# Causal mask and row minima of one attention head: two instructions over 512 columns in place of four with accumulators

## The reference, cut to what matters

```python
scores = jnp.einsum('bqnd,bknd->bnqk', q, k) * scale
causal = jnp.tril(jnp.ones((s, s), bool))
scores = jnp.where(causal, scores, -1000000000.0)
p = jax.nn.softmax(scores, axis=-1)
attn = jnp.einsum('bnqk,bknd->bqnd', p, v).reshape(b, s, NH * VD)
```

## Time and profile before

| | |
|---|---|
| timed runs, median (all three) | 987.31 us (984.85, 987.31, 988.54) |
| profiled execution, first to last instruction | 989.1 us; what lies around it isn't shown |
| PE busy | 861.2 us, 87% of the span |
| PEld busy | 611.6 us, 62% |
| DVE busy | 794.5 us, 80%, 2309 instructions |
| ACT busy | 664.4 us, 67% |
| POOL busy | 516.8 us, 52% |

### The profile page before, as it was taken

How to read it: one execution, slowest core, us unless ns; L and a number is a source line. 1 busy time by engine, 2 the same in 40 slices (tenths; PEclk the granted TensorE clock), 3 DMA queues, 4 the chain that set the end, 5 groups by cost and what they waited for, 6 DMA issues and landing times. The chain is left out here.

```text
span 989.1 us, 24025 instructions
## 1 busy us (share of the span) xinstructions
PE 861.2 (87%) x8118; PEld 611.6 (62%) x8118; DVE 794.5 (80%) x2309; ACT 664.4 (67%) x1611; POOL 516.8 (52%) x607
## 2 busy tenths in 40 slices
PE   3476689999999898999999899998998579999971
PEld 1243346777767676676767677676765357787740
DVE  4688878888888988989998877778867767777738
ACT  3677878888888877788788676666753136666640
POOL 5778883466466463777745264211453715554540
PEclk8555559999999999999999999999999779999986
DMA  5222320101001010122000223114231534444448
GB/s 183 93 77 75 102 104 23 31 19 43 15 25 30 23 52 1 59 87 71 26 15 9 65 91 119 39 34 134 80 103 46 189 108 150 153 155 148 137 161 316
DMA packets 47493, 83.81 MB, mean 85 GB/s; under 512 B 6144, under 2 KB 36224, under 8 KB 47328
## 3 DMA queue, kind: packets, MB, share of 16 engines
q1 hardware_dynamic: 39504, 61.45, 19.7%
q0 software_dynamic: 6864, 19.80, 5.7%
q10 hardware_dynamic: 1008, 1.03, 0.3%
HBM read 52.77 MB, written 31.85 MB: 86 GB/s over the span
## 5 line engine op out<-in xcount | busy, mean ns | idle before, releaser
L668 PE MATMUL ps<-whi,ar 128*128 128x256 f16 (+1 forms) x797 | 225.9, 283 | 19.0 <-DVE ar L1764 9.4
L670 PE MATMUL ps<-whi,ar 128*128 128x256 f16 (+1 forms) x797 | 225.6, 283 | 0.0
L669 PE MATMUL ps<-wlo,ar 128*128 128x256 f16 (+1 forms) x797 | 225.6, 283 | 0.0
L1543 POOL TENSOR_TENSOR ar<-ar,sm 128x512 f32<-128x512 f32 x64 | 69.8, 1090 | 149.2 <-DVE sm L1833 149.1
L668 PE MATMUL ps<-ar 128*128 128x128 f16 (+1 forms) x768 | 117.4, 207 | 13.0 <-issue 5.3
L1458 POOL TENSOR_TENSOR sm<-sm,mhalf 128x1 f32<-128x1 f32 (+2 forms) x72 | 125.4, 1741 | 6.0
L1594 POOL DMA_INDIRECT y<-ar,idx x79 | 76.0, 962 | 88.3 <-ACT ar L1428 74.4
L669 PE MATMUL ps<-ar 128*128 128x128 f16 (+1 forms) x768 | 117.0, 206 | 0.0
L670 PE MATMUL ps<-ar 128*128 128x128 f16 (+1 forms) x768 | 117.0, 206 | 0.0
L668 PE MATMUL ps<-ar,whi 128*128 128x512 f16 x292 | 114.3, 392 | 0.2
L669 PE MATMUL ps<-ar,whi 128*128 128x512 f16 x292 | 114.2, 391 | 0.0
(11 more groups left out here) (234 smaller groups left out, 2308.0 us busy)
## 6 DMA issues: line engine op xcount, KB each, us to landing
ar<-xg SPq DMA_DIRECT2D x79, 144.0 KB
ar<-in_wall SPq DMA_DIRECT2D x16, 512.0 KB, 3.6
stg<-in_wall SPq DMA_DIRECT2D x32, 188.0 KB, 2.5
ar<-in_wall SPq DMA_DIRECT2D x8, 608.0 KB, 4.3
whi<-y SPq DMA_DIRECT2D x4, 1024.0 KB, 8.1
wlo<-y SPq DMA_DIRECT2D x4, 1024.0 KB, 16.0
xg<-in_pad SPq DMA_DIRECT2D x1, 2304.0 KB
xg<-x1d SPq DMA_DIRECT2D x4, 512.0 KB, 4.7
```

The costliest lines, as they stand in the source:

```text
L668: mm(o, l_hi, r_hi, start=start, stop=False, skip_group_check=True)
L669: mm(o, l_hi, r_lo, start=False, stop=False, skip_group_check=True)
L670: return mm(o, l_lo, r_hi, start=False, stop=stop, skip_group_check=True)
L1543: TT(pr, pr, er4.unsqueeze(2).broadcast_to([P, GB, S]), ALU.mult).then_inc(sem("p_n"), 1)
```

## The change

The four instructions with accumulators become two over all 512 columns: an addition of the mask, repeated over the four batches, and a reduction by minimum over each batch's 128 columns that writes the four columns of `nm4` at once. Between them VectorE waits for the addition by a new semaphore, `m_add`. The semaphore `mask_in` is dropped: the mask's load counts on `idn_in`, behind a wait for the two loads that count there already.

```diff
                     if p == FIRST - 1:
-                        sp.dma_start(msk[:, :], maskb).then_inc(sem("mask_in"), 16)
+                        sp.wait_ge(sem("idn_in"), 32)
+                        sp.dma_start(msk[:, :], maskb).then_inc(sem("idn_in"), 16)
...
             def a_max(g, h):
                 dve.wait_ge(sem("s_ps"), g * NH + h + 1)
                 if g == 0 and h == 0:
-                    dve.wait_ge(sem("mask_in"), 16)
-                for j in range(GB):
-                    c = slice(j * S, (j + 1) * S)
-                    last = V.tensor_tensor_reduce(bank(SB_)[:, c], bank(SB_)[:, c], msk[:, :], 1.0, -MASKED, ALU.add, ALU.min,
-                                                  nm4[:, j:j + 1])
-                last.then_inc(sem("m_neg"), 1)
+                    dve.wait_ge(sem("idn_in"), 48)
+                sc = bank(SB_).rearrange("p (j k) -> p j k", j=GB)
+                TT(sc, sc, msk[:, :].unsqueeze(1).broadcast_to([P, GB, S]), ALU.add).then_inc(sem("m_add"), 1)
+                dve.wait_ge(sem("m_add"), g * NH + h + 1)
+                V.tensor_reduce(nm4, sc, AX.X, ALU.min).then_inc(sem("m_neg"), 1)
```

## The result

The changed kernel took 995.69 us (median of six, 992.82 to 1003.18) against 987.33 us, a ratio of 1.0093 with the interval 1.0062 to 1.0123. Timed a second time, beside the last experiments, it took 999.62 us, ratio 1.0134 (1.0101 to 1.0167). It is slower by about 1%. The profiled execution spans 996.1 us, and 1.9 us lie around it (997.98 us in all).

What follows compares the result with a forecast made beforehand. TensorE was taken to bound the attention stage, paying only where it waits for VectorE work behind the step: 3.8 + 1.4 + 1.1 + 1.6 + 0.6 = 8.5 us, added to the 987.31 median, gives 995.8 us; range 986.5 to 1004.

Steps and rivals of the forecast that it cites:

- The step's price: Each head's mask-and-minimum step: VectorE held 1.34 us instead of 0.96 (0.38 more), minima ready 0.32 us later.
- VectorE not the bound: Attention stage: TensorE sets the pace; 24.3 us more VectorE work over 64 heads, against 86 us of VectorE idle time.
- Late k waits: Last 20 heads: ten k projections waiting for the value split behind the step each grow by 0.38 us, 3.8 us.
- early third heads: Eleven third heads among the first 44: k projection has 0.25 us of cover, 0.13 comes through each, 1.4 us.
- late fourth heads: Fourth heads of the last five periods: value projection behind the q split starts 0.33 us later each, 1.6 us.
- Starts of periods behind the router: Heads 24, 40, 56: scores wait for the k split behind the router's softmax; all 0.38 us comes through, 1.1 us.
- Smaller places: A k/v row ahead of the query projection and a few value projections: 0 to 2 us together, taken as 0.6.
- The rival in which VectorE binds: First 440 us: delays add up, plus collisions; two thirds to all of 24.3 us paid, 1003 to 1012 us; chance 0.12.
- Hidden: Rival: pauses are given back at TensorE's later waits, so no change, 987.3 us give or take 1.5; chance 0.17.
- Faster: Rival: the two passes take 0.35 us each, the step saves 0.30 us, total 984 us; chance 0.09.
- The mask's load at nothing: Mask load on another semaphore, behind loads that ended early: SP's queue not held, cost nothing.
- The later softmax at nothing: Softmax behind the minima 0.32 us late, normalised rows needed a head later: cost nothing; without that cover up to 20 us.

Runs made afterwards that it cites:

- Runs 3 and 8: One unread VectorE reduction (0.33 us) added behind the mask-and-minimum step: in the kernel before, 991.45 us; in the changed kernel, 1009.50 us.
- run 3: The kernel before with one unread VectorE reduction over 256 mask columns added behind its four accumulating instructions: 991.45 us, ratio 1.0053.
- run 8: The changed kernel with one unread VectorE reduction over 256 mask columns added behind the changed step: 1009.50 us, ratio 1.0227.
- run 5: The kernel before with only the mask's load changed, counted on the identity's semaphore behind its two earlier loads: 987.64 us, ratio 1.0005.
- runs 9 and 10: Changed kernel, value split ahead of the mask step: in second and third heads of the last five periods, 993.27 us; also in earlier periods' third heads, 991.68 us.

## Why the prediction was right

995.8 was forecast and 995.69 measured, by the mechanism forecast: VectorE holds TensorE up where something that TensorE needs is queued behind the longer step. That the two agree to 0.1 us is luck. The second timing is 12.9 us above the kernel before, the twelve executions of both timings together (median 997.3) some 10, and the traces step by step give about 12 to 13, where 8.5 was forecast. Two places that go with the change, the query projection and `1:cat`, were sized at next to nothing and measured 6.0 us together; a term that was forecast at 1.1 did not come, and most of the steps under "all else" differ between executions anyway.

*The step's price* (1.34 us held in place of 0.96, minima 0.32 later): right, 1.34 on the trace. *VectorE not the bound*: right. *Late k waits, early third heads, late fourth heads* (6.8 us in three terms): 6.5 measured. For the third heads the rows that answer to the earlier trace rows are

```profile
320.64 0.61 PE L858 MATMUL ps<-cs,ar 128*128 128x128 f32 x4
...
322.93 0.39 PE L669 MATMUL ps<-ar,whi 128*128 128x512 f16 x1
```

2.29 us from the transposes to the projection, 2.16 before: 0.13 comes through, as the cover of 0.25 said. Runs 3 and 8 show the mechanism, and that the cover is that large.

*Starts of periods behind the router, 1.1 us: wrong*, the term is -0.35. The order on VectorE and on TensorE that answers to the earlier trace rows:

```profile
376.95 0.69 DVE L1826 TENSOR_TENSOR ps<-ps,msk 128x512 f32<-128x512 f32 x1
...
379.06 0.68 DVE L1800 SCALAR_TENSOR_TENSOR ar<-ps,ar 128x512 f16<-128x512 f32 x1
379.65 0.22 DVE L1715 TENSOR_TENSOR ar<-ps,ar 128x64 f16<-128x64 f32 x1
...
380.84 0.42 DVE L1938 TENSOR_TENSOR ar<-ar 128x64 f32<-128x64 f32 x1
...
385.11 0.68 DVE L1800 SCALAR_TENSOR_TENSOR ar<-ps,ar 128x512 f16<-128x512 f32 x1
```

```profile
385.89 0.22 PE L669 MATMUL ps<-ar 128*128 128x128 f16 x1 [1.35 <-issue]
```

and the same two steps in the kernel before, behind the first:

```profile
375.61 0.68 DVE L1799 SCALAR_TENSOR_TENSOR ar<-ps,ar 128x512 f16<-128x512 f32 x1
376.36 0.22 DVE L1714 TENSOR_TENSOR ar<-ps,ar 128x64 f16<-128x64 f32 x1
...
377.55 0.63 DVE L1938 TENSOR_TENSOR ar<-ar 128x64 f32<-128x64 f32 x1
```

From the step to the k split it is 8.16 us in both (373.88 to 382.04, 376.95 to 385.11). I had read "without a pause" as "without slack". The pair of L1799 and L1714 had 0.16 us of slack (0.75 us from start to start, now 0.59), and L1938, which reads SBUF alone, was stretched by 0.21 us more than it is now beside a subtraction of GpSimd's (376.95 to 378.11 before, 380.02 to 381.18 now; L1938 ends 0.07 to 0.08 us after it in both). Together they took in the 0.38. The pause that was to grow from 1.57 to about 1.95 us fell to 1.35.

*Smaller places, 0 to 2 us, taken as 0.6: mis-sized.* They held "a k/v row ahead of the query projection", and that alone measured 3.80. VectorE, GpSimd and TensorE in the changed kernel at the first of the three:

```profile
356.22 1.43 DVE L1740 SCALAR_TENSOR_TENSOR ar<-x,sm,cs 128x256 f32<-128x256 f32 x1
357.57 0.41 DVE L1649 SCALAR_TENSOR_TENSOR ar<-ps,cs 128x256 f32<-128x256 f32 x1
```

```profile
356.22 1.16 POOL L1508 TENSOR_TENSOR ar<-ar 128x512 f16<-128x512 f32 x1
```

```profile
358.04 0.28 PE L669 MATMUL ps<-wah,ar 128*128 128x256 f16 x1 [0.98 <-DVE ar L1649]
```

and in the kernel before, first VectorE, then GpSimd:

```profile
354.22 0.47 DVE L1739 SCALAR_TENSOR_TENSOR ar<-x,sm,cs 128x256 f32<-128x256 f32 x1
354.61 0.41 DVE L1648 SCALAR_TENSOR_TENSOR ar<-ps,cs 128x256 f32<-128x256 f32 x1
```

```profile
354.58 1.16 POOL L1507 TENSOR_TENSOR ar<-ar 128x512 f16<-128x512 f32 x1
```

Before, VectorE came 0.36 us ahead of GpSimd and took 0.47 us. The step of 0.38 us more puts both at 356.22, and VectorE's instruction lasts until 357.65, 0.27 us after GpSimd's end. I had priced a delay of 0.38 us by how near TensorE stood; what it cost in three batches was a collision of about 1 us (1.43 - 0.47) on top of it. The Trainium skill, "SBUF — State Buffer", Who interferes with whom, says that a VectorE instruction with two SBUF inputs contends with a GpSimd instruction that reads SBUF, and that the shared ports are an exclusive lock; these rows agree, in that VectorE's instruction ends only 0.27 us after GpSimd's. The rival in which VectorE binds did name such collisions, but as an addition to something else.

*`1:cat`, 2.2 us, was nowhere in the prediction: a term put at nothing without a reason.* It is the same loop, with the instruction that TensorE needs standing further back. `1:cat` (L716, now L717) waits for a subtraction (L1714, now L1715) that is the fifth VectorE instruction behind the fourth head's step. VectorE and then TensorE, before:

```profile
215.94 0.29 DVE L1826 CUSTOM_DVE_ANT_0 ps<-ps,msk 128x128 f32<-128x128 f32 x1
...
218.42 0.23 DVE L1714 TENSOR_TENSOR ar<-ps,ar 128x64 f16<-128x64 f32 x1
```

```profile
218.79 0.61 PE L716 MATMUL ps<-idn,ar 128*128 128x128 f16 x8 [0.36 <-DVE ar L1714]
```

and after:

```profile
215.83 0.69 DVE L1826 TENSOR_TENSOR ps<-ps,msk 128x512 f32<-128x512 f32 x1
...
218.53 0.21 DVE L1715 TENSOR_TENSOR ar<-ps,ar 128x64 f16<-128x64 f32 x1
```

```profile
218.89 0.61 PE L717 MATMUL ps<-idn,ar 128*128 128x128 f16 x8 [0.57 <-DVE ar L1715]
```

From the step to the subtraction it is 2.48 us before and 2.70 after: 0.22 of the 0.38 comes through, since the pair of splits and subtraction has the same 0.16 us of slack as above, and TensorE's pause grows by as much. In seven periods it is this 0.21 to 0.22, in two, without the slack, 0.36; the tenth waits for something else. Runs 3 and 8 bear it out: of the 0.33 us added, 0.17 comes through in most periods of run 3 (1.4 us in all), and all 0.33 in run 8, where the change has used the slack up (2.8). The kernel before showed the wait of 0.36 us already, so it could have been priced.

*The rivals.* Hidden: excluded, since no waits elsewhere took in the ten late ones and the stage grew by 11.8 us. Faster: excluded by 0.69 us for each pass; the two passes saved, which were weighed there, did not decide, for the reason given. The mask's load at nothing: right, run 5. The later softmax at nothing: right for the change; in runs 9 and 10, where the exchange makes it later still, VectorE waits for it and some 1.4 us are lost beside that wait.

## What to carry to other kernels

Price an instruction on a busy engine by what stands queued behind it: here 0.38 us in each of 64 heads was paid in full ten times, in full or in part in some 25 other places, and hardly elsewhere. Look past the instruction that follows at once: here the fifth behind the step held TensorE too. A small delay on VectorE also moves every later instruction against GpSimd's: look for pairs with SBUF inputs that pass within a few tenths of each other before calling a delay small. Before putting a consumer ahead of other work, see whether its producer has finished by then; the work ahead of it may be what covered that wait.

## What was not expected of the hardware

- A VectorE instruction of two SBUF inputs, 256 columns: 0.47 us ahead of a GpSimd subtraction, 1.43 us when both start together, 1.18 us when it starts 0.25 us behind it; the last two end 0.27 and 0.28 us after GpSimd does.
- Within the attention stage two profiles of one kernel agree to 0.02 us at every k projection and every query projection (3.80 and 3.79 us for the three waits), while whole executions of the changed kernel spread over 10 us (992.8 to 1003.2), those of the kernel before over 5 in the same set (984.5 to 989.3) and over 8 in a later one (981.7 to 990.1).
